# Making the last product of each tile on ScalarE and GpSimd, one step later, instead of on VectorE

## The reference

```python
h = tok(x)                                  # patches of 16, silu MLP to 512, plus a linear residual
h = h + attn(layernorm(h))                  # 16 heads of width 16, over the 64 tokens of a row; W_out, b_out
h = h + ffn(layernorm(h))                   # real(ifft(fft(z) @ w)) + bias, w complex 256 x 256
```

## Time and profile before

| | |
|---|---|
| median of 3 runs | 148.73 us (148.66 to 148.88) |
| the profiled execution | 149.01 us |
| its span, first to last instruction | 147.2 us |
| TensorE | 131.7 us busy, 89%, granted clock 1.000 |
| VectorE | 117.8 us busy, 80% |
| ScalarE | 88.1 us busy, 60% |
| GpSimd | 89.5 us busy, 61% |

### The profile page before, as it was taken

How to read it: one execution, slowest core, us unless ns; L and a number is a source line. 1 busy time by engine, 2 the same in 40 slices (tenths; PEclk the granted TensorE clock), 3 DMA queues, 4 the chain that set the end, 5 groups by cost and what they waited for, 6 DMA issues and landing times.

```text
span 147.2 us, 6094 instructions
## 1 busy us (share of the span) xinstructions
PE 131.7 (89%) x2434; PEld 113.2 (77%) x2434; DVE 117.8 (80%) x350; ACT 88.1 (60%) x248; POOL 89.5 (61%) x160
## 2 busy tenths in 40 slices
PE   0099899999999999999899999999999999999872
PEld 0098899999988877868678787897898887887641
DVE  0747964879977469899998989989989889889671
ACT  4478475747969475837558476486495594663310
POOL 6020999998230015879786786865776766673351
PEclk9999999999999999999999999999999999999999
DMA  4567000021000001102112012022131131121102
GB/s 63 161 162 254 4 0 0 0 25 17 2 0 4 0 9 20 18 25 33 46 19 58 32 26 52 8 58 47 13 60 43 14 58 40 18 53 42 33 10 71
DMA packets 24492, 5.89 MB, mean 40 GB/s; under 512 B 20368, under 2 KB 24208, under 8 KB 24464
## 3 DMA queue, kind: packets, MB, share of 16 engines
q1 hardware_dynamic: 24176, 5.40, 17.3%
q10 hardware_dynamic: 288, 0.10, 0.3%
HBM read 2.35 MB, written 2.10 MB: 30 GB/s over the span
## 4 chain that ended last, share of the span: by engine, by line
PE 57%; DVE 19%; issue 12%; POOL 4%; ACT 3%; DMA 2%; POOLq 0%; DVEq 0%
PE bank L946 9%; PE bank L932 6%; PE bank L887 6%; DVE rowmax L744 5%; PE bank L1007 3%; PE bank L985 3%; PE bank L891 3%; PE bank L974 3%; PE bank L990 2%; PE bank L1028 2%; DMA xs<-in_x 2%; PE bank L959 2%; DVE hid_lo L631 2%; PE bank L874 2%; PE bank L1041 2%
## 5 line engine op out<-in xcount | busy, mean ns | idle before, releaser
L744 DVE TENSOR_REDUCE rowmax<-bank 128x4 f32<-128x256 f32 x64 | 22.7, 418 | 5.6 <-ACT pT L371 5.3
L371 ACT ACTIVATE pT<-bank 128x256 f32<-128x256 f32 x64 | 19.4, 390 | 2.5 <-PE bank L959 2.5
L497 POOL TENSOR_SCALAR xblk<-xh,parity_sb 128x128 f32<-128x128 f32 x32 | 11.5, 371 | 14.3 <-PE bank L990 14.3
L946 PE MATMUL bank<-qT,xzT 32*128 32x64 f32 x512 | 17.9, 276 | 0.0
L946 PEld LDWEIGHTS bank<-qT,xzT 32*128 32x128 f32 x512 | 15.7, 186 | 2.7 <-issue 2.7
L631 DVE TENSOR_TENSOR hid_lo<-hidT,hid_hi 128x512 fp32r<-128x512 f32 x16 | 12.2, 761 | 5.6 <-ACT hidT L338 5.5
L366 ACT ACTIVATE maxT<-bank 128x128 fp32r<-128x128 f32 x16 | 4.4, 277 | 19.8 <-PE bank L968 19.8
L532 POOL TENSOR_TENSOR side_lo<-sideT,side_hi 128x256 fp32r<-128x256 f32 x14 | 10.2, 730 | 9.5 <-ACT sideT L381 9.5
L538 POOL TENSOR_TENSOR on_lo<-onT,on_hi 128x256 fp32r<-128x256 f32 x14 | 10.3, 735 | 7.2 <-ACT on_hi L385 7.0
L505 POOL TENSOR_TENSOR hb_all<-h_all,bout_bc 128x256 f32<-128x256 f32 x16 | 12.4, 789 | 0.0
L361 ACT ACTIVATE qT<-bank 128x256 f32<-128x256 f32 x16 | 6.2, 388 | 9.9 <-PE bank L1052 9.9
(11 more groups left out here) (152 smaller groups left out, 388.5 us busy)
## 6 DMA issues: line engine op xcount, KB each, us to landing
out<-y SPq DMA_DIRECT2D x16, 128.0 KB, 1.7
xblk<-xh SPq DMA_DIRECT2D x32, 32.0 KB, 2.2
wo_raw<-in_W_o SPq DMA_DIRECT2D x1, 512.0 KB, 3.7
wout_raw<-in_W_out SPq DMA_DIRECT2D x1, 256.0 KB, 3.0
fr<-in_wr SPq DMA_DIRECT2D x1, 256.0 KB, 4.3
fi<-in_wi SPq DMA_DIRECT2D x1, 256.0 KB, 4.3
xs<-in_x SPq DMA_DIRECT2D x1, 128.0 KB, 3.3
minus_raw<-in_minus_rows SPq DMA_DIRECT2D x1, 128.0 KB, 2.2
```

The source lines that it names most:

```text
L371: nc.scalar.activation(pT[:, j, :], bank[j][:, D:2 * D], ACT.Exp).then_inc(exp_done, 1)
L744: nc.vector.tensor_reduce(rowmax[:, j, :], bank[j][:, 0:D].rearrange("p (h k) -> p h k", k=TOK), AX_X, ALU.max).then_inc(max_done, 1)
L946: pe.matmul(bank[j][:, at0:at0 + TOK], xzT[t % 3][rows32, 2 * half + b, :, :].rearrange("p e k -> p (e k)"), qT[t % 3][rows32, half, TOK * ...
```

## The change

For tiles 0 to 13, ScalarE multiplies the product in PSUM by rstd2 and writes it to a new SBUF tile, mixed (one buffer); GpSimd adds h2b to it and writes y. Both do so at step t + 2, where VectorE did it in one instruction at step t + 1. ScalarE has it as the first instruction of its step, and it waits for rstd2, for the product, for h2 of the next tile, and for the GpSimd add of the tile before. GpSimd has its add behind place_same. SyncE stores tile t at step t + 2, behind the crossed copies. Tiles 14 and 15 stay on VectorE. The waits that guarded y, h2b, rstd2 and the PSUM half now look at the two new semaphores, mixed_set and y_added. The diff:

```diff
--- before.py
+++ after.py
@@ -158,6 +158,7 @@
         ve2 = sb("ve2", [P, 1])
         rstd2 = [sb(f"rstd2_{i}", [P, 1]) for i in range(2)]
         y = [sb(f"y{i}", [P, D]) for i in range(2)]
+        mixed = sb("mixed", [P, D])
 
         bank = [ctx.enter_context(nc.psum_tensor(f"bank{i}", [P, 512], F32)) for i in range(8)]
         bank16 = [b[:].bitcast(BF16) for b in bank]
@@ -216,6 +217,7 @@
         proj_done, h2_done = sem("proj_done"), sem("h2_done")
         stats2_done, mv2_done, ve2_done, rstd2_done = sem("stats2_done"), sem("mv2_done"), sem("ve2_done"), sem("rstd2_done")
         h2b_done, freq_done, y_set = sem("h2b_done"), sem("freq_done"), sem("y_set")
+        mixed_set, y_added = sem("mixed_set"), sem("y_added")
         y_stored = [sem("y_stored0"), sem("y_stored1")]
 
         x_tok = a["x"].rearrange("b (n f) -> (b n) f", f=PATCH).rearrange("(t p) f -> p t f", p=P)
@@ -272,7 +274,10 @@
             sp.dma_start(fbias_bc[:], a["bias"].partition_broadcast(P)).then_inc(bias_loaded, 16)
 
             def store(t):
-                sp.wait_ge(y_set, t + 1)
+                if t < WHOLE_SIDE:
+                    sp.wait_ge(y_added, t + 1)
+                else:
+                    sp.wait_ge(y_set, t + 1 - WHOLE_SIDE)
                 sp.dma_start(out_tok[:, t, :], y[t % 2][:]).then_inc(y_stored[t % 2], 16)
 
             def place_crossed(t):
@@ -292,7 +297,9 @@
             for i in range(T + 1):
                 if i + 2 < T:
                     place_crossed(i + 2)
-                if i >= 1:
+                if 2 <= i < WHOLE_SIDE + 2:
+                    store(i - 2)
+                if i > WHOLE_SIDE:
                     store(i - 1)
             for par in range(2):
                 sp.wait_ge(y_stored[par], 16 * (T // 2))
@@ -391,7 +398,18 @@
                 nc.scalar.activation(mix_whole[:].rearrange("p c n -> p (c n)"), bank[MIXW_BANK][:], ACT.Copy,
                                      scale=1.0 / D).then_inc(mix_kept, 1)
 
+            def scale_mixed(t):
+                act.wait_ge(rstd2_done, t + 1)
+                act.wait_ge(freq_done, t + 1)
+                act.wait_ge(h2_done, t + 2)
+                if t >= 1:
+                    act.wait_ge(y_added, t)
+                nc.scalar.activation(mixed[:], bank[FREQ_BANK][:, D:2 * D], ACT.Copy,
+                                     scale=rstd2[t % 2][:]).then_inc(mixed_set, 1)
+
             def step(i):
+                if 2 <= i < WHOLE_SIDE + 2:
+                    scale_mixed(i - 2)
                 if i + 1 < T:
                     copy_max(i + 1)
                 if i >= 1:
@@ -507,14 +525,21 @@
             def inv_std2(t):
                 pool.wait_ge(ve2_done, t + 1)
                 if t >= 2:
-                    pool.wait_ge(y_set, t - 1)
+                    pool.wait_ge(mixed_set, min(t - 1, WHOLE_SIDE))
                 nc.gpsimd.tensor_tensor(rstd2[t % 2][:], ve2[:], half_neg[:, 0:1], ALU.pow).then_inc(rstd2_done, 1)
 
             def add_bias(t):
                 if t >= 2:
-                    pool.wait_ge(y_set, t - 1)
+                    pool.wait_ge(y_added, t - 1)
                 pool.wait_ge(h2_done, t + 1)
                 nc.gpsimd.tensor_tensor(h2b[t % 2][:], h2[t % 2][:], fbias_bc[:], ALU.add).then_inc(h2b_done, 1)
+
+            def add_mixed(t):
+                if t >= 2:
+                    pool.wait_ge(y_stored[t % 2], 16 * (t // 2))
+                pool.wait_ge(h2b_done, t + 1)
+                pool.wait_ge(mixed_set, t + 1)
+                nc.gpsimd.tensor_tensor(y[t % 2][:], mixed[:], h2b[t % 2][:], ALU.add).then_inc(y_added, 1)
 
             def normalize(t):
                 pool.wait_ge(shift1_done, t // GROUP + 1)
@@ -540,6 +565,8 @@
             def step(i):
                 if i + 2 < T:
                     place_same(i + 2)
+                if 2 <= i < WHOLE_SIDE + 2:
+                    add_mixed(i - 2)
                 if 1 <= i <= WHOLE_SIDE:
                     split_side(i - 1)
                 if i < WHOLE_ON:
@@ -994,8 +1021,10 @@
 
             def mix_freq(t):
                 pe.wait_ge(side_copied, t + 1)
-                if t >= 1:
-                    pe.wait_ge(y_set, t)
+                if 1 <= t <= WHOLE_SIDE:
+                    pe.wait_ge(mixed_set, t)
+                elif t >= 1:
+                    pe.wait_ge(y_set, t - WHOLE_SIDE)
                 if t >= WHOLE_SIDE:
                     for half in range(HALF):
                         last = pe.matmul(bank[FREQ_BANK][:, D:2 * D], sideT[:, half * P:(half + 1) * P], mix_whole[:, half, :],
```

## The result

The changed kernel took 150.40 us (median of 6 runs, 149.77 to 150.65) against 148.91 for the kernel before (6 runs, 148.66 to 149.44); the ratio is 1.0082, interval 1.0056 to 1.0107. When both were run again, the changed one had 149.93 (12 runs) and the ratio was 1.0045 (1.0017 to 1.0072). The kernel before, run as c1 against its own other 35 runs, came out at a ratio of 0.9973 (0.9947 to 0.9998), so a difference of 0.3% between two sets is not to be trusted. Both ratios of the change lie above 1, and it makes the kernel slower, by about 0.9 us. The prediction was 148.95, with a range that ended at 149.6.

A forecast was written before the change was run, and what follows sets the result against it. Steps were taken as set by GpSimd's alignment holding VectorE's small L753, near TensorE's floor of 5.6 us. Terms 0 + 0 + 0 - 0.05 + 0.28 = +0.23 on 148.73 gave 148.95 us; range 147.6 to 149.6.

The forecast's parts named there:

- DVE removed: VectorE loses 14 L780 (6.6 us busy); freed time becomes idle ahead of L711: 0, bounds 0 and 4.7 us.
- ACT, covered: ScalarE's added product fits its idle time between h2 and maxT, with 0.15 to 0.3 us left: 0.
- POOL in the regular steps: GpSimd's 0.73 us add fits the idle time between xblk and side_lo; everything behind on_lo keeps its place: 0.
- POOL in step 2: No idle time there: the add makes side_lo about 0.5 us later, hidden in TensorE's wait for h2: -0.05.
- SP, +0.28: SyncE's crossed copies leave earlier, xh is never late, so L753 is held in two more later steps: +0.28 us.
- End, 0: Tiles 14 and 15 keep L780; tile 13's product and add fall where ScalarE and GpSimd wait: 0.
- The sum against the median: Whole kernel: +0.23 us applied to the median of 148.73, with 1.8 us around the span: 148.96, rounded to 148.95.
- Case 3: GpSimd's add holds VectorE's inv_rows inside divide; h2b and hb_all slip 0.15 in four steps: 149.55 us, chance 0.11.

The follow-up runs named there:

- c1: The kernel before, unchanged, run again: 148.88 us (12 runs).
- e4: The kernel before, with y of tiles 0 to 13 not made at all and h2b stored instead: 149.13 us, ratio 1.0003.
- e11: The kernel before, with hb_all moved into GpSimd's idle time, xh waiting for L753, and no y for tiles 0 to 13: 146.49 us (2 runs).
- e6: The changed kernel, with each tile's ScalarE product made twice, once to a spare tile nobody reads: 150.41 us, ratio 1.0102.
- e5: The changed kernel, with tile 0 left to VectorE, so step 2 has neither GpSimd's add nor ScalarE's product: 149.16 us, ratio 1.0012.
- e10: The kernel before, with each store of y issued one step later, behind the next crossed copies: 149.37 us, ratio 1.0033.

## Why the prediction was wrong, step by step

- *DVE removed, worth 0.* Right to within 0.3 us: e4 and e11 show it, and the idle time went where it was said.
- *ACT, covered.* Right: mixed starts 0.17 behind h2 (0.05 had been taken) and maxT 0.70 behind. With 0.37 from one product to the next instruction, as in e6, 0.16 is left of the 0.15 to 0.3 forecast, and e6 shows the end of the cover.
- *POOL in the regular steps, covered.* Right: side_lo starts behind the add, on_lo keeps its 0.57.
- *POOL in step 2, -0.05 with bounds -0.2 and +0.3.* This step failed. Measured +0.19 to +0.47, mean 0.37; six of the eight profiles lie above the upper bound (0.42 to 0.47). The rows of steps 2 and 3 of the changed kernel:

```profile
68.29 0.74 POOL L542 TENSOR_TENSOR y<-mixed,h2b 128x256 f32<-128x256 f32 x1
...
68.98 0.73 POOL L557 TENSOR_TENSOR side_lo<-sideT,side_hi 128x256 fp32r<-128x256 f32 x1
...
69.77 0.51 PE L1040 MATMUL bank<-mix_hi,side_lo 128*128 128x256 f32 x2 [0.45 <-POOL side_lo L557]
...
72.31 0.55 POOL L550 TENSOR_SCALAR xh<-h_all,rstd,shift 128x256 f32<-128x256 f32 x1
...
72.91 0.44 PE L1070 MATMUL bank<-ident,xh 128*128 128x128 f32 x2
...
75.29 1.21 ACT L378 ACTIVATE pT<-bank 128x256 f32<-128x256 f32 x4 [0.28 <-PE bank L986]
...
77.00 0.73 POOL L523 TENSOR_TENSOR hb_all<-h_all,bout_bc 128x256 f32<-128x256 f32 x1
...
77.23 0.53 DVE L778 CAST max_terms<-rowmax 128x16 fp32r<-128x16 f32 x1
...
77.79 0.20 DVE L780 TENSOR_TENSOR max_terms<-rowmax,max_terms 128x16 fp32r<-128x16 f32 x1
```

  The first half came as worked out: the add (68.29) pushes side_lo to 68.98 and L1040 (L1011 before) to 69.77, and h2 was early. What I left out is that POOL's lateness runs on through its whole step: xh starts at 72.31, and L1070, the turn of xh for step 3, waits for it until 72.91. That is 0.35 behind the start of the turn before it (L995), where in the regular step it follows by 0.11 (84.65 and 84.76). pT comes late (75.29, with ACT idle 0.28 before it), and now the splits fall on the next hb_all: L778 takes 0.53 (it is the L751 of before, with 0.17 in the regular steps) and ends 0.03 behind it. In this profile, one of the two cheap ones (0.19 and 0.20), L780 then gets through in 0.20. In the other six it takes 0.49 to 0.50, beside xh. I had looked at who waits for side_lo and for h2, not at everyone who waits for GpSimd. e5 takes the add out of step 2, and the two steps are 12.36 again.
- *SP, +0.28.* Right in its first half only. xh is never late (1.93 to 1.95 behind on_lo in all eight profiles), as said. But the forecast took it that L753 is then held in all of steps 6 to 11, and it is held in 3 to 5 of them, against 4, 2 and 1 before. In steps where xh starts 0.11 to 0.13 ahead of L753, as it now always does, both outcomes occur. Against the profile on which the forecast was worked out, with its four held steps and 39.72, the mean after is 39.69, so the +0.28 did not come. Against the mean of the three profiles before it is +0.21, and their ranges overlap.
- *End, 0.* Right.
- *The sum against the median, 1.8 us around the span taken as fixed.* This failed too: it is 2.14 in the changed kernel, 0.34 more, and its cause stays open. The starting point was low as well: 148.73 was the median of three runs, and the mean of 47 is 149.10.

So of the 0.9 us some 0.4 is a term of the sum with the wrong size and 0.34 a term that was missing. The remaining 0.2 lies where the forecast had put its 0.28, but within what profiles of one kernel differ by.

Case 3 was not it: inv_rows stayed at 0.45 in all profiles. In twelve of the thirteen steps of the changed kernel in which it ran beside the add, it had started 0.02 to 0.31 ahead of it; in one the add was running first:

```profile
140.27 0.72 POOL L542 TENSOR_TENSOR y<-mixed,h2b 128x256 f32<-128x256 f32 x1 [1.32 <-ACT mixed L407]
...
140.75 0.45 DVE L790 STREAM_TRANSPOSE inv_rows<-inv_sum 128x256 f32<-128x256 f32 x1
```

By the Trainium skill, GPSIMD Engine Reference, Key points, GpSimd contends with VectorE instructions that have two SBUF inputs; the trace agrees, since L753 was held and inv_rows, with one SBUF input, was not. But the cast L778 has one SBUF input too and took 0.53 instead of 0.17 beside hb_all, so by the rows of this case two inputs are not the only thing that decides.

The range was also too narrow above because it took one execution's timing (clock rise at 10.9, which is early) as the kernel's.

## What to carry to other kernels

Before work is moved to a less busy engine, list every instruction behind the new one in its queue up to the next idle time, and everyone who waits for them; a step without idle time (here step 2) is where a covered instruction turns up in the sum. A busy share of 80% said nothing: removing 6.6 us from that engine gave nothing that the times show, while putting one tiny instruction out of reach of its neighbour on another engine, with that neighbour's work moved into idle time, gave 1.8 us. Compare several profiles of the same kernel before a difference in one stretch is believed.

## What the runs showed of the hardware that I had not expected

TensorE's granted clock rose to 2.4 GHz between 10.7 and 13.7 us after the start, from one execution to the next, with TensorE at work from 7.4 to 7.8 on in all of them. With a rise before 11.3 the steps started 0.8 us earlier on the mean than with one behind 13.0.

The time outside the span differed by 0.34 between programs (1.80 and 2.14) and was the same in each execution of nearly every program. Of four additions to one engine's list, only that on ScalarE's moved it.

A VectorE instruction of 16 elements with two SBUF inputs took 0.60 to 0.67 us beside one GpSimd instruction (hb_all) and 0.44 to 0.50 beside another (xh), instead of 0.17 (0.80 once, in e6). It ended 0.01 to 0.04 behind that GpSimd instruction wherever it was held in the profiles of before, after and e10. From step 6 on, with xh started 0.06 to 0.09 ahead of it or behind it, it took 0.17 to 0.20 in every profile. With xh started 0.11 to 0.13 ahead, it came out at 0.17 or 0.18 in some steps and at 0.44 to 0.46 in others, so the starts alone, to 0.01 us, don't tell which it will be.
